# Half-width matmul tiles and a new order of calls in a gated-delta attention kernel

## The reference

```
x = x + 0.5 * ffn(layernorm(x))        # 8 experts, each token goes to its best 2
x = x + attention(layernorm(x))
x = x + 0.5 * ffn(layernorm(x))
```

```
A   = I + tril((K*b) @ K.T, -1);   T = inv(A)
mid = T @ (V*b) - T @ (K*b) @ S.T          # inverse by values
O   = Q @ S.T + (Q @ K.T * tril) @ mid     # outputs
S   = S + mid.T @ K                        # state growth
```

## Time and profile before

| what | value |
|---|---|
| three runs | 1599.9, 1599.24, 1593.64 us, median 1599.24 |
| profiled execution | 1593.92 us, its span 1592.2 us |
| PE, weight loads, DVE, ACT, POOL busy | 83%, 78%, 70%, 58%, 63% of the span |
| attention stage | from about 392 us to about 1316 us |
| steps before the gate starts (491.77 to 593.91 us) | 4 steps in 102.14 us |
| steps with the gate (700.09 to 1125.65 us) | 16 steps in 425.56 us |

### The profile page before, as it was taken

How to read it: one execution, slowest core, us unless ns; L and a number is a source line. 1 busy time by engine, 2 the same in 40 slices (tenths; PEclk the granted TensorE clock), 3 DMA queues, 4 the chain that set the end, 5 groups by cost and what they waited for, 6 DMA issues and landing times. The chain is left out here.

```text
span 1592.2 us, 36649 instructions
## 1 busy us (share of the span) xinstructions
PE 1325.0 (83%) x11688; PEld 1241.4 (78%) x11688; DVE 1119.1 (70%) x2788; ACT 918.2 (58%) x1853; POOL 998.5 (63%) x1812
## 2 busy tenths in 40 slices
PE   7773994994589999999999999999999841995996
PEld 7663994994478888888888888888888741994996
DVE  6574772673768788879888888797887534673674
ACT  2123772771356676767676767676767423772773
POOL 4772673575366676777776867877768532575466
PEclk8556996998789999999999999999999965997999
DMA  7437976672011212132222231322222245875792
GB/s 212 154 108 190 312 256 223 233 252 69 11 30 39 51 46 75 40 74 76 63 67 58 62 77 35 79 72 67 68 56 62 62 143 157 267 265 190 251 291 75
DMA packets 224024, 195.88 MB, mean 123 GB/s; under 512 B 105556, under 2 KB 186714, under 8 KB 223840
## 3 DMA queue, kind: packets, MB, share of 16 engines
q1 hardware_dynamic: 190560, 117.21, 26.8%
q0 software_dynamic: 24576, 67.94, 11.7%
q10 hardware_dynamic: 8704, 8.39, 1.8%
HBM read 103.68 MB, written 96.10 MB: 125 GB/s over the span
## 5 line engine op out<-in xcount | busy, mean ns | idle before, releaser
L1557 DVE SCALAR_TENSOR_TENSOR raw_w<-attn_raw,taps,raw_w 128x256 f32<-128x256 f32 x576 | 249.0, 491 | 58.6 <-ACT raw_w L1928 58.6
L468 PE MATMUL ffn_both<-ws,ffn_xhi 128*128 x1152 | 204.3, 289 | 0.4
L468 PEld LDWEIGHTS ffn_both<-ws,ffn_xhi 128*128 128x128 f32 x1152 | 164.8, 192 | 2.8 <-issue 2.8
L457 PE MATMUL ffn_both<-ident,ffn_xb 128*128 128x128 f32 x576 | 82.0, 290 | 94.7 <-ACT ffn_xb L752 94.7
L2210 POOL TENSOR_TENSOR attn_inv<-attn_inv,attn_term 64x14 f32<-64x14 f32 (+6 forms) x448 | 136.5, 305 | 35.1
L2207 POOL TENSOR_TENSOR attn_term<-attn_small,attn_inv 64x14 f32<-64x14 f32 (+6 forms) x448 | 131.1, 293 | 32.6
L1199 PE MATMUL attn_fr<-attn_xhi,wqkv 128*128 128x256 f32 x768 | 148.0, 295 | 2.5 <-DVE attn_xlo L1537 1.6
L457 PEld LDWEIGHTS ffn_both<-ident,ffn_xb 128*128 128x128 f32 x576 | 70.1, 150 | 97.1 <-ACT ffn_xb L752 76.9
L491 PE MATMUL ffn_yb<-ws,ffn_hhi 128*128 x576 | 119.9, 292 | 6.2 <-DVE ffn_hlo L667 6.2
L1199 PEld LDWEIGHTS attn_fr<-attn_xhi,wqkv 128*128 128x128 f32 x768 | 112.5, 193 | 14.1 <-issue 10.6
L829 POOL DMA_INDIRECT second_rows<-ffn_more_rows,ffn_to x64 | 63.1, 986 | 85.3 <-DVE ffn_to L652 69.3
(11 more groups left out here) (317 smaller groups left out, 4051.1 us busy)
## 6 DMA issues: line engine op xcount, KB each, us to landing
ffn_more_rows<-second_rows SPq DMA_DIRECT2D x56, 259.0 KB
ffn_xb<-second_rows SPq DMA_DIRECT2D x48, 259.0 KB
raw_w<-second_rows SPq DMA_DIRECT2D x40, 259.0 KB
ffn_more_rows<-first_rows SPq DMA_DIRECT2D x64, 131.0 KB
ffn_xb<-in_L_attn_x_dram SPq DMA_DIRECT2D x8, 1024.0 KB, 5.9
attn_xin<-x_after_first ACTq DMA_DIRECT2D x32, 256.0 KB, 2.7
attn_xres<-x_after_first SPq DMA_DIRECT2D x32, 256.0 KB, 3.0
x_after_attention<-attn_xres SPq DMA_DIRECT2D x32, 256.0 KB
```

The costliest lines, as they stand in the source:

```text
L457: last = pe.transpose(tr[:, q, j * P:(j + 1) * P], xs[:, k % 2, j, q * P:(q + 1) * P], ident[:])
L468: last = pe.matmul(hp[:, j, :], (xhi, xlo)[b][:, k % 2, q, j * P:(j + 1) * P], ws[:, bass.ds(experts[j], 1), a, q].rearrange("p o d -> p ( ...
L1557: dve.scalar_tensor_tensor(acc[:, j, r], raw[:, j, r, :, tap:tap + P], taps[:, j, r, tap:tap + 1], acc[:, j, r], ALU.mult, ALU.add)\
```

## The change

`mids`, `outputs` and `state_out` computed 128 columns where only 64 were wanted: each head's 128x128 inverse multiplied the values of two heads, and only the matching half was kept. Now each product is split in two of 64 output partitions (rows 0 to 63 and 64 to 127 of the tile, `c` = 0, 1) and 64 columns. There are twice as many matmuls, each a quarter of the size; `mid` becomes dense and half as large, and `mid_out` copies one contiguous piece. It is no longer zeroed. Beside that the lists of calls of all five engines have another order, and `gate_stats` gets a wait on its own earlier result.

```
-        mid = sb("mid", [P, 2, H, P])
+        mid_room = sb("mid", [P, 2, H, P])
+        mid = mid_room[:, 0].rearrange("p h t -> p (h t)").rearrange("p (s h d) -> p s h d", s=2, h=H)
...
             def mids(st):
-                        last = pe.matmul(sc[:, s, h * P:(h + 1) * P], inverses[par % 2][:, s, h, :], vn[:, par, s, r * P:(r + 1) * P],
-                                         start=(h == 0), stop=True, skip_group_check=True)
+                        d = slice(h * D, (h + 1) * D)
+                        for c in range(2):
+                            a = slice(c * D, (c + 1) * D)
+                            last = pe.matmul(sc[a, s, d], inverses[par % 2][:, s, h, a], vn[:, par, s, d],
+                                             start=(h == 0), stop=True, skip_group_check=True)
...
             def outputs(st):
+                        for c in range(2):
+                            a = slice(c * D, (c + 1) * D)
+                            last = pe.matmul(ob[a, s * DM + h * D:s * DM + (h + 1) * D], at[:, par, s, h, a],
+                                             mid[:, s, h, :], start=False, stop=True, skip_group_check=True)
...
             def state_out(st):
+                        for c in range(2):
+                            h = 2 * r + c
+                            last = pe.matmul(sc[c * D:(c + 1) * D, s, r * D:(r + 1) * D],
+                                             ktok[:, par, s, h * D:(h + 1) * D], mid[:, s, h, :],
+                                             start=(r == 0), stop=True, skip_group_check=True)
...
             def mid_out(st):
+                    act.activation(mid[:, s].rearrange("p h d -> p (h d)"), sc[:, s, 0:DM], ACT.Copy).then_inc(mid_ready[s], 1)
```

More of the change, by code:

```diff
@@ L1160, in body @@
             def body(f, g, t, s, u, v):
+                if s:
+                    load_residual(s)
                 if g:
@@ L1163, in body @@
                     take_blocks(g)
[L1164 to L1167, removed]
+                if s and isinstance(s[0], int) and (s[0] == NS - 1):
+                    load_weights()
                 if s:
@@ L1463, in body @@
                 if s:
+                    state_in(s, v)
                     out_in(s)
-                    state_in(s, v)
                 if g:
                     gram(g, 1)
-                if f:
-                    qkv(f, 0)
                 if s:
@@ L1472, in body @@
                     outputs(s)
+                    state_out(s)
+                if f:
+                    qkv(f, 0)
                 if t:
@@ L1507, in body @@
                     turn_back(f)
+                if s:
+                    out_project(s)
             steps_of(pe, body)
@@ L1806, in clear_buffers @@
                     dve.memset(state[:, s], 0.0).then_inc(s_ready[s], 1)
-                for buf in (mid[:], n16[:], i16[:], i32[:], *inverses, n32[:]):
+                for buf in (n16[:], i16[:], i32[:], *inverses, n32[:]):
                     dve.memset(buf, 0.0).then_inc(zeroed, 1)
@@ L1817, in body @@
             def body(f, g, t, s, u, v):
-                more = f and not (isinstance(f[0], int) and f[0] + 1 >= NS)
+                more = f and (not (isinstance(f[0], int) and f[0] + 1 >= NS))
                 if g:
@@ L1827, in body @@
                 if f:
+                    x_low(f)
                     history(f)
@@ L1878, in body @@
                         clear_buffers()
+                if t and isinstance(t[0], int) and (t[0] == 0):
+                    column_sums_out()
+                if u:
+                    gate_stats(u)
+                if s:
+                    out_low(s)
+                if v and v[1] == 2:
+                    gate_sums(v)
+                if v and v[1] == 1:
+                    gate_first(v)
+                if f:
+                    norms(f)
                 if u:
                     gate_products_out(u, v)
-                if v and v[1] == 1:
-                    gate_first(v)
                 if s:
                     residual(s)
-                if t and isinstance(t[0], int) and t[0] == 0:
-                    column_sums_out()
-                if f:
-                    norms(f)
             steps_of(dve, body)
@@ L2088, in body @@
                     gate_turned(u)
+                if f:
+                    silus(f, 0)
                 if t:
@@ L2258, in body @@
                     gate_scatter(v, 3, GB)
+                if v and v[1] == 1:
+                    gate_pow(v)
                 if more:
                     inverse_std(f[0] + 1)
-                if v and v[1] == 1:
-                    gate_pow(v)
                 if s:
```

112 lines of the change are left out of this document (45 added, 67 removed).

## The result

The changed kernel takes 1605.31 us (median of 20 runs, 1596.33 to 1611.01), the kernel before 1598.01 (20 runs, 1593.64 to 1602.43). The ratio is 1.0046, 95% interval 1.0034 to 1.0057: slower by half a per cent, 7.3 us, against a forecast of 1586. Of each kernel one execution was profiled, and these two lie further apart: the changed kernel's took 1610.45 us, 5 more than its median, and the one of before 1593.92, 4 less than its median. Their spans are 1608.6 and 1592.2 us. What follows is read from these two, so it shows where 16.4 us went, more than twice the difference of the medians.

A forecast was written before the change was run, and what follows sets the result against it. PE looked like the bound, but the SP-POOL loop (24.5 us against 25.54) limits gains. From the profiled 1593.92: 8 steps x 0.25 = 2, 21 gate steps x 0, 8 at the end, so 1584; forecast 1586, range 1574 to 1597.

The forecast's parts named there:

- The tiles: PE's `mids`, `outputs`, `state_out`: 80 half-width records take 2.6 us instead of 4.45, saving 1.85 us per step.
- the rival that the halves don't work at once: Column halves take turns on PE: 2.4 us more ahead of `qkv`, 20 us longer, 1612; chance 0.07.
- The loop bounds the steps: SP collects inverses, spreads and takes blocks, POOL inverts: 24.5 us per turn before, 25.1 after, limiting what PE's savings bring.
- the four early steps take 25.3 us each as worked out: Steps without gate work: a chain of 24.6 and a loop of 25.1 settle at 25.3 us, against 25.54.
- The residual load in the loop, +0.6: SP's `load_residual` between collecting and spreading lengthens the loop from 24.5 to 25.1 us per turn.
- Once a batch `load_batch`, two issues and 1.0 us, stands there too: SP's batch load between collecting and spreading adds 1.0 us to the loop once a batch.
- The rival "loop slower": Residual's and store's 256 KB delay small transfers by about 1 us each; turn 26.9, 30 us slower, 1624; chance 0.16.
- pairs of more than 12 us: From SP's collecting issue to `take_blocks`: over 12 us, against a mean of 10.6, would show the slower loop.
- The wait of 3.2 us behind the three scatters: PE at `mids`, once a batch: values arrive late after POOL's scatters, with no `qkv` ahead to cover it; 3.2 us.
- The end of the stage, 8 us: Earlier weights and scatters bring the batch load and last scatters forward: 8 us gained, bounds 3 and 11.
- In the last three steps ... 1 us: In the last three steps `state_in` no longer waits for `residual` through `out_in`: 1 us gained.
- The rule of the Trainium skill that I weighed in the prediction: On PE, weight loads overlap running matmuls only where the row group differs; by it the 80 records would take 4.8 us.

The follow-up runs named there:

- the batch load back: The changed kernel with `load_batch` alone moved back to right behind `take_blocks`: 1592.71 us, ratio 0.9965 to the kernel before.
- the quarter of its bytes: The changed kernel with the batch load in its new place but loading only 64 of its 256 columns: 1596.58 us, ratio 0.9996 to the kernel before.

## Why the prediction was wrong

- **The tiles**: right. 2.9 us against 2.6 taken, 4.45 before; the rival that the halves don't work at once is out.
- **The loop bounds the steps**: right. POOL waits for `attn_small` in 13 of 17 steps, and `x_turn` waits no more. From one end of the inversion to the next POOL takes, in the four steps of a batch from the one with the scatters on, 30.2, 25.0, 28.5 and 25.1 us (means of four batches); the prediction's sum was 29.9, 25.1, 26.1 and 25.1. Only the one with the batch load is off. That the four early steps take 25.3 us each as worked out is in part luck, since the traces of two other kernels with the same code there (the batch load back, the quarter of its bytes) give 25.6.
- **The residual load in the loop, +0.6**: right in size, 0.4 to 0.7 in the pairs; from `attn_r<-small_inverses_turned` to the first small block it is 1.8 us with it and 1.2 without. By the medians it is worth 13 us (1605.3 against 1592.2), but the batches show only 0.2 to 0.3 us a step of it (108.6 against 107.9, and 106.6 against 105.4 without the batch load). Where the rest comes from stays open.
- **"Once a batch `load_batch`, two issues and 1.0 us, stands there too"**: this is the step that failed. I priced the issues and put at nothing what the transfer does to the small ones behind it. The issues took 1.2 us, and the blocks landed 1.5 us later besides; the pair grew by 2.7 to 2.8 us and POOL's turn from 26.1 to 28.5 (28.5 also in the one shown, 844.34 to 872.84). Since `mids` has no cover in the new order, PE stood 4.23 us and then ran at the lower clock for part of the step. A batch was 108.6 us instead of 106.6, and with the load back behind the blocks it was 106.64, in a kernel 12.6 us faster. The rival "loop slower" had the mechanism, 256 KB ahead of blocks of 8 KB, but laid it on the residual in every step; it was the batch load, 1 MB in two issues, once a batch. The prediction's own sign for it, pairs of more than 12 us, came.
- **The wait of 3.2 us behind the three scatters**: wrong place. PE waits 0.32 us there (905.90), and 4.23 one step earlier; the late step before it had moved everything else back.
- **The lower clock**: not in the prediction at all. Before, the steady steps showed none of it, and I added PE's waits as if they cost only their own length. In the step above it kept PE busy some 3.6 us longer, 1.6 of them in the 80 records.
- **The end of the stage, 8 us**: right, -7.9, from the last store to the end of the last scatter; 3.4 of it goes with the early weights, in two traces.
- **"In the last three steps ... 1 us"**: wrong, +6.6: 2.5 in the last step with a `turn_back` and 4.1 in the drain. In the drain no `qkv` fills PE's waits, and in the new order the products of the inverse stand ahead of the output's turn and product; but that order is not what made it longer. The three kernels with full-width tiles drain in 63.9 to 65.0 us, the one with the new order (65.0) among them, at a mean clock of 0.92 or 0.93; the ten with half-width tiles take 66.2 to 71.2 at 0.78 to 0.87, the two with the old order (66.7 and 68.2) among them. So the longer drain goes with the tiles: they leave PE less to do where it already waits, and what it saves it gives back at the lower clock (50.4 us busy before, 51.4 after). That the clock is the whole reason is my reading.

The forecast's own range, 1574 to 1597, missed; only the outer one, 1560 to 1616, held the time. The sign was wrong: 0.55 stood on faster. Two terms were off, the batch load's and the last steps'. The sum of the rival on the halves is 21 us by its own terms and not 20, which changes nothing.

## What to carry to other kernels

Price a DMA that is moved ahead of small, awaited ones by what it does to their landing, not by its issues alone: 1 MB in front of 64 KB cost 2.7 us here, not 1.0. Before moving two things at once, ask whether one takes the cover from the other: the two loads cost about 7 us in the kernel before and 22 beside the other new orders. A wait of PE of 4 us or more was paid for twice in these traces, since what followed ran at the lower clock. And compare terms, not only totals: one profiled execution can lie 5 us from its kernel's median, as it did here.

## What the runs showed of the hardware

- Products of 128 rows by 64 columns in alternating output halves come every 0.036 us, full-width ones of 128 columns every 0.111. Work split so is cheaper by a third for the same result (80 records in 2.9 us, 40 in 4.45), though both halves share all their rows. The rule of the Trainium skill that I weighed in the prediction (TensorE: Matmul & The Clock Gate, The mechanism, in Part 3) does not hold for this pair: weight loads of the same rows start while a record runs (906.010 and 906.016, within 906.007 to 906.229).
- Two loads of 512 KB in front of eight small stores and one small load lengthened their way through DRAM by 2.7 to 2.8 us, 1.5 of them between the last small store and its landing. With a quarter of the bytes and as many rows it was 1.5 in all (12.8 against 11.3 for the other pairs of that kernel), and nothing at the landing (1.9 and 1.9).
- The drain, in which PE waits a good deal, had a mean granted clock of 0.92 or 0.93 in the three kernels with full-width tiles and of 0.78 to 0.87 in the ten with half-width ones, and was 1.2 to 7.3 us longer in these.
